# Cross-attention and feed-forward layer: normalised x and the attention weights are turned by DMA transposes instead of by TensorE

## The reference

```python
x = x + xattn(layernorm(x), ctx, ctx, mask, Wq, Wk, Wv, wq_h, ..., Wo)
x = x + ffn(layernorm(x), w1, b1, w2, b2)
# xattn: scores = qh @ kh.T / 4, masked, softmax over 64, @ vh, tiled 16 times, @ Wo
# ffn:   gelu(x @ binarize(w1).T + b1) @ binarize(w2).T + b2
```

## Time and profile before

| | |
|---|---|
| Time, median of 3 runs (lowest to highest) | 397.78 us (395.81 to 399.18) |
| Profiled execution: time, span of its instructions | 397.82 us, 396.0 us |
| Busy: PE, DVE, ACT, POOL | 340.2, 333.1, 259.5, 312.6 us (86, 84, 66, 79% of the span) |
| Mean granted clock of PE | 0.954 of full speed |
| DMA traffic | 21.39 MB, mean 54 GB/s |

### The profile page before, as it was taken

The page is one execution under the profiler, slowest core; times in us unless marked ns, Lnnn a source line. Parts: engine busy times, 40 slices in busy tenths (PEclk is TensorE's granted clock), DMA queues, the critical chain, the costliest instruction groups (busy, mean ns, idle before and its releaser), DMA issues. The chain is left out here.

```text
span 396.0 us, 7941 instructions
## 1 busy us (share of the span) xinstructions
PE 340.2 (86%) x2387; PEld 230.0 (58%) x2387; DVE 333.1 (84%) x722; ACT 259.5 (66%) x486; POOL 312.6 (79%) x460
## 2 busy tenths in 40 slices
PE   5888979999797997979888979798897988889793
PEld 3544645758474756656564747474655656465562
DVE  1978889999799897989898979889898989897555
ACT  1078276788685776776767668587676776768370
POOL 1304739769989899898898898989899899886856
PEclk9975569999999999999999999999999999999898
DMA  8800101010202011111102020201011111001012
GB/s 261 290 2 1 54 0 55 2 54 2 106 2 105 4 57 49 53 53 53 53 29 77 0 106 0 106 0 67 38 53 53 53 53 53 0 0 55 0 55 106
DMA packets 9424, 21.39 MB, mean 54 GB/s; under 512 B 1720, under 2 KB 4928, under 8 KB 9408
## 3 DMA queue, kind: packets, MB, share of 16 engines
q1 hardware_dynamic: 8496, 21.14, 14.8%
q10 hardware_dynamic: 912, 0.05, 0.2%
HBM read 12.80 MB, written 8.39 MB: 54 GB/s over the span
## 5 line engine op out<-in xcount | busy, mean ns | idle before, releaser
L649 DVE SCALAR_TENSOR_TENSOR h_lo<-h_sb,h_scale,h_hi 128x512 f16<-128x512 f32 x128 | 113.4, 915 | 11.2 <-POOL h_hi L419 7.0
L1234 PE MATMUL psZ<-sgn2T,h_hi 128*128 128x256 f16 x512 | 117.8, 275 | 0.5 <-DVE sgn2T L868 0.2
L1234 PE MATMUL psZ<-sgn2T,h_lo 128*128 128x256 f16 x512 | 117.5, 275 | 0.0
L498 ACT ACTIVATE h_sb<-psY,b_col,alpha1x 128x512 f32<-128x512 f32 x128 | 94.7, 777 | 8.5 <-PE psY L1220 5.9
L1220 PE MATMUL psY<-x_hi,sgn1T 128*128 128x512 f16 x256 | 97.6, 381 | 1.6 <-ACT sgn1T L621 1.6
L1220 PE MATMUL psY<-x_lo,sgn1T 128*128 128x512 f16 x256 | 97.5, 381 | 0.0
L419 POOL TENSOR_SCALAR h_hi<-h_sb,h_scale 128x512 f16<-128x512 f32 x64 | 48.2, 757 | 21.9 <-PE psZ L1234 19.7
L409 POOL TENSOR_SCALAR xh<-x,rstd,nmr 128x256 f32<-128x256 f32 x64 | 62.6, 990 | 3.4 <-issue 1.9
L1170 PE MATMUL psW<-ident,xh 128*128 128x128 f32 x256 | 36.4, 288 | 31.4 <-POOL xh L409 31.4
L1234 PEld LDWEIGHTS psZ<-sgn2T,h_hi 128*128 128x128 f16 x512 | 50.4, 98 | 13.9 <-DVE h_lo L649 5.2
L442 POOL TENSOR_TENSOR z_sb<-z_sb,x1b 128x256 f32<-128x256 f32 x62 | 56.5, 941 | 0.0
(11 more groups left out here) (151 smaller groups left out, 524.0 us busy)
## 6 DMA issues: line engine op xcount, KB each, us to landing
x_in<-in_x SPq DMA_DIRECT2D x16, 512.0 KB, 3.4
out_x<-z_sb SPq DMA_DIRECT2D x15, 512.0 KB, 2.6
w_sb<-in_L_ffn_w SPq DMA_DIRECT2D x2, 1024.0 KB, 9.5
ctx_sb<-in_ctx SPq DMA_DIRECT2D x1, 1024.0 KB, 6.7
out_x<-z_sb SPq DMA_DIRECT2D x2, 256.0 KB, 2.2
wk_sb<-in_L_xattn_Wk SPq DMA_DIRECT2D x1, 256.0 KB, 3.2
wq_sb<-in_L_xattn_Wq SPq DMA_DIRECT2D x1, 256.0 KB, 3.6
wv_sb<-in_L_xattn_Wv SPq DMA_DIRECT2D x1, 256.0 KB, 7.1
```

The costliest lines, as they stand in the source:

```text
L498: nc.scalar.activation(h_sb[c % 4][:, :], psY[c % 4][:, :], ACT.Gelu, bias=b1_col[:, c:c + 1], scale=alpha1x[:, c:c + 1]) \
L649: nc.vector.scalar_tensor_tensor(out=h_lo[c % 4][:, :], in0=h_sb[c % 4][:, :], scalar=h_scale[:, :], in1=h_hi[c % 4][:, :], op0=ALU.mult, ...
L1234: last = nc.tensor.matmul(psZ[j // 2][:, (j % 2) * D:(j % 2 + 1) * D], part[c % 4][:, j * P:(j + 1) * P], sgn2T[:, c, :], start=(c == 0 an ...
```

## The change

ScalarE rounds xh[0], as it lies in SBUF, to a new float16 tile xh_hi, and VectorE subtracts to xh_lo, each in one instruction of 1024 elements a partition. SP then issues a DMA transpose of each (128 x 1024, 256 KB) into xT_hi and xT_lo, which now have the tile index ahead of the half index. e_hl is likewise turned by one DMA transpose (128 KB) straight into eT. turn_x for n = 0, turn_e and the eT copy go away. In SP's body the transpose of e of n + 1 comes first, then the load of x, then the two transposes of xh of n + 2, then the store. TensorE's score waits for both transposes, attend for that of e. GpSimd waits with the next xh[0] for the split, no longer for the turn.

```diff
+            def turn_xh(i, par):
+                wait_apart(sp, scored, val(i, par - 1, 1, 1))
+                wait_apart(sp, xh_hi_done, val(i, par, 1, 1))
+                sp.dma_start(xT_hi[:, :, :, :].rearrange("p j k t -> p (j k) t"),
+                             xh_hi[:, :, :].rearrange("p j d -> p (j d)"), transpose=True) \
+                  .then_inc(xT_hi_turned, 16)
+                wait_apart(sp, xh_split, val(i, par, 1, 1))
+                sp.dma_start(xT_lo[:, :, :, :].rearrange("p j k t -> p (j k) t"),
+                             xh_lo[:, :, :].rearrange("p j d -> p (j d)"), transpose=True) \
+                  .then_inc(xT_lo_turned, 16)
+
+            def turn_e(i, par):
+                wait_apart(sp, attended, val(i, par - 1, 2, 2))
+                wait_apart(sp, e_split, val(i, par, 1, 1))
+                sp.dma_start(eT[:, :, :], e_hl[:, :, :, :].rearrange("p j n t -> p (j n t)"),
+                             transpose=True).then_inc(e_turned, 16)
...
+            turn_xh(0, 0)
             def body(i, par):
+                if has(i, par + 1):
+                    turn_e(i, par + 1)
                 if has(i, par + 3):
                     wait(sp, x1_ready, val(i, par + 1, 1, 1))
                     load_x(i, par + 3)
+                if has(i, par + 2):
+                    turn_xh(i, par + 2)
...
-                wait(pool, (x_turned, x1_turned)[n], val(i, par - 1, KD, KD))
+                if n == 0:
+                    wait(pool, xh_split, val(i, par - 1, 1, 1))
+                else:
+                    wait(pool, x1_turned, val(i, par - 1, KD, KD))
...
-            def copy_xT(i, par):
-                wait(act, scored, val(i, par - 1, 1, 1))
-                for k in range(KD):
-                    wait(act, x_turned, val(i, par, KD, k + 1))
-                    nc.scalar.activation(xT_hi[:, k, :], psW[k][:, :], ACT.Copy,
-                                         scale=X_SCALE).then_inc(xT_hi_copied, 1)
+            def round_xh(i, par):
+                wait(act, xT_hi_turned, val(i, par - 1, 16, 16))
+                wait(act, normed[0], val(i, par, 1, 1))
+                nc.scalar.activation(xh_hi[:, :, :], xh[0][:, :, :], ACT.Copy,
+                                     scale=X_SCALE).then_inc(xh_hi_done, 1)
...
-                if late:
-                    wait(act, e_turned, val(i, par + 1, 1, 1))
-                    wait(act, attended, val(i, par, 2, 2))
-                    nc.scalar.activation(eT[:, :, :].rearrange("p j t -> p (j t)"),
-                                         psW[0][:, :].bitcast(F16)[:, 0:T * P], ACT.Copy) \
-                        .then_inc(eT_copied, 1)
...
-            def split_xT(i, par):
-                for k in range(KD):
-                    wait(dve, xT_hi_copied, val(i, par, KD, k + 1))
-                    nc.vector.scalar_tensor_tensor(out=xT_lo[:, k, :], in0=psW[k][:, :], scalar=X_SCALE,
-                                                   in1=xT_hi[:, k, :], op0=ALU.mult,
-                                                   op1=ALU.subtract).then_inc(xT_copied, 1)
+            def split_xh(i, par):
+                wait(dve, xT_lo_turned, val(i, par - 1, 16, 16))
+                wait(dve, xh_hi_done, val(i, par, 1, 1))
+                nc.vector.scalar_tensor_tensor(out=xh_lo[:, :, :], in0=xh[0][:, :, :], scalar=X_SCALE,
+                                               in1=xh_hi[:, :, :], op0=ALU.mult,
+                                               op1=ALU.subtract).then_inc(xh_split, 1)
...
             def score(i, par):
-                wait(pe, xT_copied, val(i, par, KD, KD))
+                wait(pe, xT_hi_turned, val(i, par, 16, 16))
+                wait(pe, xT_lo_turned, val(i, par, 16, 16))
+                wait(pe, x1_ready, val(i, par - 1, 1, 1))
...
             def attend(i, par):
-                wait(pe, eT_copied, val(i, par, 1, 1))
+                wait(pe, e_turned, val(i, par, 16, 16))
                 wait(pe, lo_copied, val(i, par - 1, KD, KD))
-                wait(pe, xT_copied, val(i, par, KD, KD))
+                wait(pe, e_split, val(i, par, 1, 1))
...
-                if late:
-                    turn_e(i, par + 1)
...
-                if early:
-                    turn_x(i, par + 2, 0)
```

More of the change, by code:

```diff
@@ L155, in xattn_ffn_kernel @@
         xh = [sb(f"xh{n}", [P, T, D]) for n in range(2)]
-        xT_hi = sb("xT_hi", [P, KD, S], F16)
-        xT_lo = sb("xT_lo", [P, KD, S], F16)
+        xh_hi = sb("xh_hi", [P, T, D], F16)
+        xh_lo = sb("xh_lo", [P, T, D], F16)
+        xT_hi = sb("xT_hi", [P, T, KD, P], F16)
+        xT_lo = sb("xT_lo", [P, T, KD, P], F16)
         sc = sb("sc", [P, T, SK])
@@ L247, in xattn_ffn_kernel @@
         normed = [sem(f"normed{n}") for n in range(2)]
-        x_turned = sem("x_turned")
-        xT_hi_copied = sem("xT_hi_copied")
-        xT_copied = sem("xT_copied")
+        xh_hi_done = sem("xh_hi_done")
+        xh_split = sem("xh_split")
+        xT_hi_turned = sem("xT_hi_turned")
+        xT_lo_turned = sem("xT_lo_turned")
         scored = sem("scored")
@@ L259, in xattn_ffn_kernel @@
         e_turned = sem("e_turned")
-        eT_copied = sem("eT_copied")
         attended = sem("attended")
@@ L488, in exp @@
                 wait(act, exped, val(i, par, 1, 1))
-                wait(act, e_turned, val(i, par - 1, 1, 1))
+                wait(act, e_turned, val(i, par - 1, 16, 16))
                 nc.scalar.activation(e_hl[:, :, 0, :], e_sb[:, :, :], ACT.Copy,
@@ L547, in _ @@
             copy_values(0)
-            copy_xT(0, 0)
+            round_xh(0, 0)
             act.wait_ge(mv_scales_ready, 1)
@@ L599, in body @@
                 if early:
-                    copy_xT(i, par + 2)
+                    round_xh(i, par + 2)
                 if is_body(i, par, -1):
@@ L821, in _ @@
             dve.wait_ge(mv_scales_ready, 1)
-            split_xT(0, 0)
+            split_xh(0, 0)
             for m, (k, n) in enumerate((k, n) for n in range(NH) for k in range(KD)):
@@ L952, in body @@
                 if early:
-                    split_xT(i, par + 2)
+                    split_xh(i, par + 2)
                 if is_body(i, par, 0):
@@ L1153, in sum_alpha2, with turn_x1 @@
                 last.then_inc(pe_alpha2, 1)
[L1155 to L1166, removed]
+            def turn_x1(i, par):
+                wait(pe, normed[1], val(i, par, 1, 1))
+                wait(pe, x1_ready, val(i, par, 1, 1))
+                for k in reversed(range(KD)):
+                    if k == 0 and has(i, par + 1):
                         wait(pe, sc_steps, val(i, par + 1, 3, 2))
@@ L1170, in turn_x @@
                         last = nc.tensor.transpose(psW[k][:, j * P:(j + 1) * P],
-                                                   xh[n][:, j, k * P:(k + 1) * P], ident[:, :])
-                    last.then_inc((x_turned, x1_turned)[n], 1)
+                                                   xh[1][:, j, k * P:(k + 1) * P], ident[:, :])
+                    last.then_inc(x1_turned, 1)
             def score(i, par):
-                wait(pe, xT_copied, val(i, par, KD, KD))
+                wait(pe, xT_hi_turned, val(i, par, 16, 16))
+                wait(pe, xT_lo_turned, val(i, par, 16, 16))
+                wait(pe, x1_ready, val(i, par - 1, 1, 1))
                 for j in range(T):
@@ L1178, in score @@
                         last = nc.tensor.matmul(psW[0][:, j * 2 * SK:(j + 1) * 2 * SK],
-                                                part[:, k, j * P:(j + 1) * P],
+                                                part[:, j, k, :],
                                                 M_hl[:, k, i * 2 + par, :, :].rearrange("p n t -> p (n t)"),
@@ L1182, in score, with attend @@
                 last.then_inc(scored, 1)
-            def turn_e(i, par):
+            def attend(i, par):
+                wait(pe, e_turned, val(i, par, 16, 16))
+                wait(pe, lo_copied, val(i, par - 1, KD, KD))
                 wait(pe, e_split, val(i, par, 1, 1))
-                wait(pe, lo_copied, val(i, par - 1, KD, KD))
-                ps = psW[0][:, :].bitcast(F16)
-                for j in range(T):
-                    last = nc.tensor.transpose(ps[:, j * P:(j + 1) * P],
-                                               e_hl[:, j, :, :].rearrange("p n t -> p (n t)"),
-                                               ident16[:, :])
-                last.then_inc(e_turned, 1)
-            def attend(i, par):
-                wait(pe, eT_copied, val(i, par, 1, 1))
-                wait(pe, lo_copied, val(i, par - 1, KD, KD))
-                wait(pe, xT_copied, val(i, par, KD, KD))
                 for j in range(T):
@@ L1297, in body @@
                 if late:
-                    turn_x(i, par + 1, 1)
+                    turn_x1(i, par + 1)
                 if ffn:
@@ L1314, in _ @@
             pe.wait_ge(b1_copied, 1)
-            turn_x(0, 0, 0)
             turn_mags()
```

## The result

| | Before | After |
|---|---|---|
| Time, median (lowest to highest) | 397.73 us (395.81 to 399.18), 4 runs | 435.53 us (434.03 to 438.05), 4 runs |
| Profiled execution: time, span | 397.82, 396.0 us | 435.88, 433.8 us |
| Mean granted clock of PE | 0.954 | 0.903 |

The ratio is 1.096, with a 95% interval of 1.089 to 1.103: slower, by 37.8 us. The sign was forecast and the size was not: the forecast was 475 us, 77 us of loss, just over twice as much as came, though 435.5 lies inside the range of 412 to 600.

A forecast was written before the change was run, and what follows sets the result against it. GpSimd's chain was taken as the bound at 21.27 us; landing 19.7 plus 5.1, clock 1.5 and e path 0.1 made a period of 26.4. Then 397.8 + 71 (14 bodies x 5.1) + 6 = 475 us, range 412 to 600.

The forecast's parts named there:

- What bounds the kernel before: GpSimd's own work, closed through TensorE's turn of x1 and second product of chunk 3, sets the 21.27 us period.
- The removed work: 0 us: Transposes and copies taken from TensorE, ScalarE and VectorE lie off the loop, so removing them gains 0 us a period.
- Landing of xT_lo plus 5.1: New period: landing X of xT_lo plus 5.1 us through score, second products, turn of x1; X = 19.7 gives 24.8.
- the second way to be wrong: The wait before attend, not the one before the score, becomes the long one.
- T = 2.3 us for 256 KB: Queue time of each x transpose, geometric middle of 0.73 and 7.2 us, with 1.5 us of issue and completion round it.
- The clock, 1.5 us a period on the path: TensorE idles some 4 us before the score, its clock falls, and 1.5 us a period is lost; bounds 0 and 3.
- The e path, 0.1 us: Attend starts 2.9 us later, delaying gelus and rounding; between 0 and 1.2 us a period, 0.1 taken.
- The prologue and the end, 6 us: Unpipelined transpose latency: about 1.2 us first score, 1.2 first e, 3 batch 1, 1 at the end; together 6.
- Plain speed: Rival: transposes as fast as plain transfers, T = 0.73, landing 2.2 us after issue, period 22.2, 413 us; chance 0.18.
- Small pieces: Rival: transposes move in 32-byte pieces at 14 ns each, T = 7.2, period 36.8, about 620 us; chance 0.20, or worse.
- the hidden case: Rival: xT_lo lands by t 16.2, GpSimd stays the bound, up to 1.3 us a period gained, 385 to 398 us; chance 0.07.

The follow-up runs named there:

- the kernel without waits: Full change, but score and attend multiply unturned data and wait for no DMA transpose, though all transposes still run; 402.61 us, ratio 1.010.
- plain copies: Full change with all three DMA transposes made plain copies of the same bytes between the same tiles, so nothing is turned; 409.02 us, ratio 1.025.
- x by TensorE: Kernel before the change, with only the transpose of e given to the DMA on SP and no eT copy; 413.35 us, ratio 1.038.

## Why the prediction was wrong

**What bounds the kernel before.** Right. GpSimd's chain was the loop: 0.7 us taken from it shortened each period by 0.8, and the removal of TensorE's transposes, with no wait put in their place (the kernel without waits), gained nothing.

**The removed work: 0 us.** Right. Rounding 1.04 us (1.35 taken) and split 1.22 (1.3 taken) were near enough. The sentence that GpSimd's work doesn't change was right for its sum in the full change (19.50 for 19.22); only where the split begins just ahead of the power does that operation grow, as in the kernel without waits.

**Landing of xT_lo plus 5.1.** Right, in the full change (241.03 to 246.13) and with the clock held (22.9 for 22.8). The mechanism forecast for the slowdown is the one that ran: a score that waits for a DMA, with second products, the turn of x1 and GpSimd's last h_hi behind it. But that wait was put at some 4 us and is 2.27; the one before attend is 3.17. This is the second way to be wrong that the prediction named, and it came true in part: the wait before attend is the longer, while the form of the sum held.

**T = 2.3 us for 256 KB: the term that was mis-sized.** From the issue of hi (236.55) to the landing of lo (241.03) are 4.48 us; with the 1.5 us round it, T = 1.49. The busy share of the DMA engines says the same: 2.96 us for both. The middle of 0.73 and 7.2 was too long by 0.8, and twice that stands in the landing: 1.6 us a period. The lower rows were the nearer ones, and the pages of the two kernels say why. Packets before and after, and the SP queue after (for the earlier trace rows):

```profile
DMA packets 9424, 21.39 MB, mean 54 GB/s; under 512 B 1720, under 2 KB 4928, under 8 KB 9408
DMA packets 51919, 31.86 MB, mean 73 GB/s; under 512 B 44216, under 2 KB 47424, under 8 KB 51904
...
q1 hardware_dynamic: 50992, 31.63, 26.8%
```

The transposes added some 42,500 packets for 10.5 MB, about 250 bytes each and not the 32 that were assumed. The queue's time went from 14.8% of 396 us to 26.8% of 433.8 on sixteen engines, 920 us more, or 22 ns a packet: an estimate of 1.4 us for 256 KB. The plain copies moved the same bytes in 6,900 packets and added 440 us, 0.7 us for 256 KB.

The Trainium skill's sentence in "Advanced Engine Details and Errata", section X-Bar Transpose (TRN2), that transposing DMAs are as fast as regular ones, isn't borne out here: 3.1 to 3.3 us against 2.3 for plain copies of the same 256 KB. Its 1309 ns for a 128 x 128 block ("VectorE: DVE Perf Modes", section The three transpose paths) can't be a rate, for eight such blocks landed in 3.1 us.

**The clock, 1.5 us a period on the path: right that it falls, wrong where.** I put it behind the wait before the score. There the clock was at full rate in the period shown, with a stall of 2.27 us; it fell behind the wait for eT, where it costs only through the late gelus. With the store at 128.37 a period of 26.9 us begins (the next is at 155.30), the one such among the ten, in which it fell at the score as well, behind a stall of 2.09 us. So the sum had 1.5 us a period too much in this place. The rows near the end of the kernel before, with a stall of 2.17 us and the clock down behind it, couldn't carry it: the same length of stall goes with either clock here.

**The e path, 0.1 us: too small.** In the full change the rounding started 0.9 us after the 12.2 that I had taken (t 13.13). I had bounded it at 1.2, and chose the wrong end: the time that ScalarE saved wasn't given back, since its gelus waited for first products that ran at half rate. Issue of xT_hi at t 14.27 instead of 13.6 is what remains after the shorter rounding: +0.7 us.

Together: 26.4 - 1.6 - 1.5 - 0.1 + 0.7 = 23.9, the period measured.

**The prologue and the end, 6 us: too much.** Fourteen bodies at the measured 2.8 us make 39 us, already 1 more than the whole loss; nothing is left for the 6. The 39.5 us by which the forecast was too high are thus 14 x 2.3 = 32 from the period (forecast 5.1 more, measured 2.8), and some 7 from this term.

**The rivals.** Plain speed (413 us) named the wrong price, and the run with plain copies shows what it would have been: 409. That the two are so near is partly luck, for the rival had periods of 22.2 us with the clock held, and the copies had periods of 21.4 with it held and of 22.5 to 23.1 where it fell. Its argument that all 256 KB transfers land in 2.2 us holds for the two stores alone; loads of that size (wk_sb, wq_sb, wv_sb) took 3.2 to 7.1 us in the same profile. Small pieces and the hidden case didn't occur; that case's 385 us doesn't follow from its own 1.3 us a period, which gives 398 - 14 x 1.3 = 380. None of the rivals had what the experiments showed most strongly, that an earlier landing of one transfer can make the kernel slower.

## What to carry to other kernels

A transpose taken from an engine that wasn't the bound gained nothing here, and since its result was wanted soon by the in-order engine that feeds the bound, what its latency had beyond the slack was paid in each period: with the clock held (by added matmuls or by itself), 1.3 us for transposes that land in 3.1 us and nothing for copies that land in 2.3. Find the closed loop first and write the period as one landing plus what stands behind it; that form survived here even where its numbers didn't. Where TensorE must wait, ask behind which wait the clock will fall and what runs there: two improvements (e taken back, the store moved behind e) made this kernel slower by moving that place onto the path, and useless matmuls made it faster.

## What the runs showed of the hardware

- A DMA transpose of 128 x 1024 in float16 (256 KB) landed 3.1 to 3.3 us after issue and kept the sixteen engines busy some 1.5 us; a plain copy of the same bytes landed in 2.3. For 128 x 512, 2.7 us behind a store on the same queue and 2.4 ahead of it, against 2.2 (behind the store).
- The transposes ran as packets of about 250 bytes, some 22 ns each on one DMA engine; the plain copies of the same bytes as packets of some 1.5 KB.
- SP is occupied 1.24 us by each transpose instruction, for 128 KB as for 256 KB, where a plain copy takes it 0.35 to 0.5 us.
- TensorE's granted clock fell to the 1.2 GHz level behind waits of 3.0 to 3.6 us (attend, in each of the ten periods of the full change) and of 5.1 us. The length of a wait alone doesn't decide it. Before the score of the full change it fell behind 2.1 us and held behind 2.2 to 2.8; with plain copies it fell behind five waits of 2.6 to 2.7 us and held behind five of 2.7 to 2.9; with x by TensorE it held behind 3.1 and fell behind 3.2 to 3.4; without waits it fell behind five waits of 1.81 us and held behind five of the same length.
- GpSimd's power over 128 x 4 elements took 1.98 us when it began just after VectorE's subtraction with two SBUF inputs, and 1.02 when it began just ahead of it.
